# A spectral filter's channel mixing moved from the whole matrix array to 64x64 tiles of it

## The reference

```
h = layer_norm(x, n1_g, n1_b)
xf = rfft2(h, axes=(1, 2), norm='ortho')          # 128 x 65 frequencies, 128 channels
xf = xf.reshape(B, H, W//2+1, 8, 16)              # 8 blocks of 16 channels
o1r = relu(xr @ w1[0] - xi @ w1[1] + b1[0])       # each block with its own 16x16 weights
o1i = relu(xi @ w1[0] + xr @ w1[1] + b1[1])
o2r = softshrink(o1r @ w2[0] - o1i @ w2[1] + b2[0])
o2i = softshrink(o1i @ w2[0] + o1r @ w2[1] + b2[1])
h = irfft2(o2r + 1j * o2i) + h + x
out = gelu(layer_norm(h, n2_g, n2_b) @ mw1 + mb1) @ mw2 + mb2 + h
```

## Time and profile before

| What | Value |
|---|---|
| Time, median of 3 runs | 1652.82 us (1651.64 to 1653.29) |
| Time of the profiled execution | 1653.2 us |
| Its span, first to last instruction | 1651.4 us |
| Mean granted TensorE clock | 1.000 |
| First filter, start of `dft_h` to start of `idft_h` | 77.67 to 170.36 us |
| Last filter | 1273.5 to 1366.3 us |

### The profile page before, as it was taken

One profiled execution on the slowest core, in us unless ns is written; L12 is line 12 of the kernel. 1 busy time (PEld: TensorE's weight loads), 2 busy tenths in 40 slices (PEclk: granted clock), 3 DMA queues, 4 the chain that ended last, 5 costly groups with the idle time before them and its releaser, 6 DMA issues.

```text
span 1651.4 us, 34968 instructions
## 1 busy us (share of the span) xinstructions
PE 1598.6 (97%) x11278; PEld 1445.4 (88%) x11278; DVE 1076.1 (65%) x2697; ACT 938.4 (57%) x1782; POOL 619.8 (38%) x774
## 2 busy tenths in 40 slices
PE   0999999999999999999999999999999999999999
PEld 0999988888999988888899998888889998888888
DVE  7889566556559856655656966665664995555453
ACT  5655276666535546666644545666663553666665
POOL 4800046766800016676660002677673000211111
PEclk9999999999999999999999999999999999999999
DMA  7500713333300062333320042333331006011111
GB/s 222 197 15 1 238 45 108 95 102 121 97 14 1 8 236 83 108 95 102 122 78 1 1 166 94 101 108 101 102 110 46 1 1 204 27 32 38 32 39 45
DMA packets 167249, 137.67 MB, mean 83 GB/s; under 512 B 9459, under 2 KB 131189, under 8 KB 167157
## 3 DMA queue, kind: packets, MB, share of 16 engines
q1 hardware_dynamic: 166354, 136.23, 26.1%
q10 hardware_dynamic: 802, 0.21, 0.1%
HBM read 69.29 MB, written 67.11 MB: 83 GB/s over the span
## 4 chain that ended last, share of the span: by engine, by line
PE 79%; DVE 14%; issue 4%; ACT 1%; SPq 1%; DVEq 1%; DMA 1%; POOL 0%; ACTq 0%
PE ps L756 27%; PE ps L558 7%; PE ps L722 7%; PE ps L724 7%; PE ps L683 7%; PE ps L723 7%; DVE vsb L1105 4%; PE ps L716 3%; PE ps L702 3%; PE ps L708 3%; DVE csb L1107 3%; DVE usb L1095 3%; DVE usb L1096 2%; PE ps L568 2%; PE ps L612 2%
## 5 line engine op out<-in xcount | busy, mean ns | idle before, releaser
L756 PEld LDWEIGHTS ps<-mw,gel 128*128 128x128 f32 x4000 | 520.6, 191 | 42.3
L756 PE MATMUL ps<-mw,gel 128*128 128x128 f32 x4000 | 523.7, 274 | 0.0
L875 ACT ACTIVATE gel<-ps,mb1f 128x512 f32<-128x512 f32 x500 | 343.7, 687 | 250.5 <-PE ps L724 219.7
L1460 POOL TENSOR_TENSOR arena<-arena,mb2rep 128x512 f32<-128x512 f32 x125 | 160.1, 1281 | 654.6 <-ACT hn L861 654.6
L722 PE MATMUL ps<-hth,mw1h 128*128 128x512 f32 x512 | 260.3, 508 | 2.9 <-DVE htl L1206 1.5
L1449 POOL TENSOR_SCALAR arena<-xnext,rstd,shift 128x128 f32<-128x128 f32 x360 | 159.3, 462 | 207.6 <-DVE shift L1344 207.6
L861 ACT ACTIVATE hn<-arena,shift,rstd 128x128 f32 (+1 forms) x512 | 221.7, 483 | 16.7 <-DVE shift L1344 16.7
L1189 DVE TENSOR_TENSOR arena<-ps,arena 128x512 f32 (+1 forms) x60 | 41.5, 691 | 252.4 <-PE ps L708 233.8
L724 PE MATMUL ps<-hth,mw1l 128*128 128x512 f32 x512 | 202.1, 395 | 0.0
L723 PE MATMUL ps<-htl,mw1h 128*128 128x512 f32 x512 | 200.8, 392 | 0.0
L846 ACT ACTIVATE osb<-usb,vectors 128x512 f32<-128x512 f32 (+1 forms) x136 | 95.6, 703 | 158.3 <-DVE usb L1096 158.3
(11 more groups left out here) (118 smaller groups left out, 2397.9 us busy)
## 6 DMA issues: line engine op xcount, KB each, us to landing
arena<-aside SPq DMA_DIRECT2D x128, 256.0 KB, 5.0
aside<-gz SPq DMA_DIRECT2D x96, 256.0 KB, 3.0
between<-xout SPq DMA_DIRECT2D x62, 256.0 KB, 2.3
out_dram<-xout SPq DMA_DIRECT2D x62, 256.0 KB, 2.3
xnext<-between SPq DMA_DIRECT2D x60, 256.0 KB, 3.1
aside<-first SPq DMA_DIRECT2D x32, 256.0 KB, 2.3
xnext<-in_x_dram SPq DMA_DIRECT2D x30, 256.0 KB, 3.1
first<-in_x_dram SPq DMA_DIRECT2D x1, 960.0 KB, 7.2
```

What stands on the lines that cost most here:

```text
L756: mm = pe.matmul(ps[:, r % 2, P * i:P * i + P], gel[:, r % 2, m, P * i:P * i + P], mw2[:, s // IMAGES, m, :], start=(m == 0 and i == 0), s ...
L875: act.activation(gel[:, r % 2, m, :], ps[:, 2 + m % 2], ACT.Gelu, bias=mb1f[:, s // IMAGES, m:m + 1]).then_inc(gelu_out, 1)
L1460: pool.tensor_tensor(t, t, b, ALU.add).then_inc(mb2_done, 1)
```

## The change

`mix1` and `mix2` take two units (both halves of the channels) at once, and each matmul uses a part of the array.

The channels are laid out anew: a half of 64 channels is split in two quarters `g` of 32, so that partitions 0 to 63 hold real and imaginary part of one quarter, and 64 to 127 those of the other. In `mix1` each of the four combinations of `q` and `g` has a stationary operand of 64x64 on a tile of the array of its own: rows `g`, columns `g ^ q`. The even and odd parts are no longer combined by VectorE. Four groups of such matmuls write the sums directly into PSUM: even to the first 65 columns, even again to the other 63, odd added to the columns 1 to 63, and odd with the other sign added to the last 63. `w1s` has four kinds of weights instead of two, for the signs.

`e_copy`, `combine`, `usb` and `nyq` go. `o_relu` reads PSUM. `mix1` of a pair waits for both relus of the pair before. In `mix2` the stationary operand is the upper or lower 64 rows of `osb` (64x128), with 64 moving columns, into banks 4 + 2 (p % 2) + `g`; the banks alternate by pair. `filter_` issues for each pair: `mix1` of the next, `mix2` of this one, two `dft_h`. Other parts: the small loads of the weights are 13 (`load_weights`) and 5 (`load_vectors`) transfers instead of 6, GpSimd builds two more kinds of weights, `scale_spectral` scales four kinds, and the evictions of `dft_w` write to the new layout.

The diff, cut to its core:

```
...
+PAIRED = UNITS // 2
+EDGE_PAIR = 4
...
-        w1s = sb("w1s", [P, 2, 2, 2, HALF])
-        w2s = sb("w2s", [P, 2, 2, HALF])
+        w1s = sb("w1s", [P, 4, 2, 2, QUART])
+        w2s = sb("w2s", [P, 2, 2, QUART])
...
-            dst = spec_of(s)[:, :, q, :, bass.ds(GROUP * cg, GROUP)]
+            dst = spec_of(s)[:, :, q, g ^ q, :, bass.ds(GROUP * cg, GROUP)]
...
+            def mix1(s, p):
+
+                alone = p == 1
                 if not alone:
+                    pe.wait_ge(g_out, 2 * BATCHES * s + spectrum_of(2 * p + 1) + 1)
+                if p:
+                    pe.wait_ge(o_out, UNITS * s + 2 * p)
+
+                def quarters(j0, j1, depth, src, dst, kind, start=False):
+
+                    for q in range(2):
+                        for g in range(2):
+                            own_rows = slice(HALF * g + depth[0], HALF * g + depth[1])
+                            cols = slice(HALF * (g ^ q), HALF * (g ^ q) + HALF)
+                            to = ps[cols, 2 + q].rearrange("p (j k) -> p j k", j=GROUP)[:, j0:j1]
+                            mm = pe.matmul(to[:, :, dst[0]:dst[1]], w1s[own_rows, kind, q].rearrange("p r c -> p (r c)"),
+                                           gsb[own_rows, q, j0:j1, src[0]:src[1]], start=start, stop=True,
                                                skip_group_check=True)
+                    return mm
+
+                def sums(j0, j1, depth, even, plus, minus, start=False):
+
+                    quarters(j0, j1, depth, (0, EVEN), (0, EVEN), even, start)
+                    quarters(j0, j1, depth, (1, KWS), (EVEN, P), even)
+                    quarters(j0, j1, depth, (EVEN, P), (1, KWS), plus)
+                    return quarters(j0, j1, depth, (EVEN, P), (EVEN, P), minus)
+
                 if alone:
+                    mm = sums(0, 1, (QUART, HALF), 1, 3, 0, True)
+                elif p:
+                    mm = sums(0, GROUP, (0, HALF), 0, 1, 2, True)
+                else:
+                    sums(1, GROUP, (0, HALF), 0, 1, 2, True)
+                    sums(0, 1, (0, QUART), 0, 1, 2)
...
+            def mix2(s, p):
+                kws = 1 if p == 1 else GROUP
...
+                if p >= 2:
+                    pe.wait_ge(v_out, UNITS * s + 2 * p - 2)
+                for q in range(2):
+                    pe.wait_ge(o_out, UNITS * s + 2 * p + q + 1)
+                    for i in range(kws):
+                        for g in range(2):
+                            own_rows = slice(HALF * g, HALF * (g + 1))
+                            at_ = 2 * HALF * 2 * q + HALF * i
+                            mm = pe.matmul(ps[:, 4 + 2 * (p % 2) + g, at_:at_ + HALF], osb[own_rows, q, i, :],
+                                           w2s[own_rows, q].rearrange("p r c -> p (r c)"), start=True, stop=True)
+                mm.then_inc(m2_mm, 2)
...
+                for p in range(PAIRED):
+                    if p + 1 < PAIRED:
+                        mix1(s, p + 1)
...
+                    mix2(s, p)
+                    if p == EDGE_PAIR:
                         edges(s)
+                    if p + 3 < PAIRED:
+                        for q in range(2):
+                            dft_h(s, 2 * p + 6 + q)
...
-            def e_copy(s, n, q, kws=GROUP):
...
-                act.activation(dst, src, ACT.Relu, bias=b1v[:, q:q + 1]).then_inc(o_out, 1)
+                act.activation(dst, ps[:, 2 + q, 0:P * kws], ACT.Relu, bias=b1v[:, q:q + 1]).then_inc(o_out, 1)
...
                 def batch(b, last=False):
                     n = 2 * b + 2
...
                     if not last:
+                        for q in range(2):
+                            g_copy(s, n + 2 + q, q)
+                    for q in range(2):
+                        o_relu(s, n + q, q)
...
-                    for kind in range(2):
+                    for kind in range(4):
...
-            def combine(s, n, q, kws=GROUP):
...
```

More of the change, by code:

```diff
@@ L527, in dc_bias @@
                 for q in range(2):
-                    mm = pe.matmul(ps[:, 7, q:q + 1], w1s[0:HALF, 0, q].rearrange("p r c -> p (r c)"),
-                                   beta64[0:HALF, q:q + 1], start=(q == 0), stop=True, skip_group_check=True)
-                mm.then_inc(dc_mm, 1)
+                    if q:
+                        pe.wait_ge(dc_mm, 2 * n + 1)
+                    for g in range(2):
+                        rows_, cols = slice(HALF * g, HALF * g + QUART), slice(HALF * (g ^ q), HALF * (g ^ q) + HALF)
+                        mm = pe.matmul(ps[cols, 7, q:q + 1], w1s[rows_, 0, q].rearrange("p r c -> p (r c)"),
+                                       beta64[q][rows_], start=(q == 0), stop=True, skip_group_check=True)
+                    mm.then_inc(dc_mm, 1)
             def evicted(s, cg):
@@ L576, in mix1 @@
                 if not alone:
[L577 to L586, removed]
@@ L602, in mix1 @@
                         mm = pe.matmul(ps[:, 2 + q, 0:1], IDENT, dcbias[:, q:q + 1], start=False, stop=True,
                                        skip_group_check=True)
[L604 to L614, removed]
+                mm.then_inc(m1_mm, 2)
@@ L625, in filter_ @@
                 mix1(s, 0)
[L626 to L640, removed]
-                        edges(s)
+                for q in range(2):
+                    dft_h(s, 4 + q)
+                for p in range(PAIRED):
+                    if p + 1 < PAIRED:
+                        mix1(s, p + 1)
+                    if p == EDGE_PAIR + 1:
+                        pe.wait_ge(y_done, (UNITS + 1) * s + 2 * EDGE_PAIR + 2)
+                    mix2(s, p)
+                    if p == EDGE_PAIR:
+                        edges(s)
+                    if p + 3 < PAIRED:
+                        for q in range(2):
+                            dft_h(s, 2 * p + 6 + q)
+                if s:
+                    fc1_held(s, 0)
+                    fc1_held(s, 1)
+                else:
+                    pe.wait_ge(v_out, UNITS * s + UNITS - 2)
+                    keep_warm(8, 6)
             def edges(s):
                 pe.wait_ge(t_edge, s + 1)
+                pe.wait_ge(v_out, UNITS * s + 2 * EDGE_PAIR)
                 for i, m in enumerate((REVERSE, IDENT)):
@@ L907, in _ @@
                 for q in range(2):
-                    with act.Fori(0, CGROUPS // 8) as j:
-                        for r in ((0, 2) if s else range(4)):
-                            a_out(s, q, j, r)
+                    for g in range(2):
+                        with act.Fori(0, CGROUPS // 16) as j:
+                            for r in ((0, 2) if s else range(4)):
+                                a_out(s, q, g, j, r)
                 if s:
@@ L1249, in _, with batch @@
                     for q in range(2):
[L1250 to L1252 removed]
+                        for g in range(2):
+                            with dve.Fori(0, CGROUPS // 16) as j:
+                                for r in (1, 3):
+                                    a_out(s, q, g, j, r)
                         if q == 0 and s % IMAGES == 0:
                             scale_spectral(s // IMAGES)
[L1255 to L1263 removed]
+                for q in range(2):
+                    shrink(s, q, 0, q, 0)
+                for q in range(2):
+                    shrink(s, 2 + q, BATCHES, q, 1, kws=1)
                 edges(s)
[L1266 removed]
+                def batch(b, odd):
                     for q in range(2):
[L1268 to L1278 removed]
+                        shrink(s, 2 * b + 2 + q, b, q, odd)
+                        if isinstance(b, int) and b + 1 == EDGE_PAIR and q == 0:
+                            edges_out(s)
+                for b in range(1, EDGE_PAIR):
+                    batch(b, (b + 1) % 2)
+                with dve.Fori(EDGE_PAIR // 2, BATCHES // 2 - 1) as i:
+                    own.enter(i, 4, EDGE_PAIR // 2)
+                    for h in range(2):
+                        batch(2 * i + h, 1 - h)
+                own.leave(BATCHES // 2 - 1)
+                batch(BATCHES - 2, 1)
+                batch(BATCHES - 1, 0)
                 dve.wait_ge(y_done, (UNITS + 1) * (s + 1))
```

174 lines of the change are left out of this document (66 added, 108 removed).

## The result

The changed kernel takes 1697.24 us (median of 4 runs, 1695.81 to 1698.33) against 1653.05 us for the kernel before (median of 4 runs), a ratio of 1.0268 with a 95% interval of 1.025 to 1.0286. It is slower by 44 us, not by the 134 us forecast. The direction was right and the range, 300 us wide, held the time, but the forecast of the size was wrong by a factor of three.

What follows compares the result with a forecast made beforehand. TensorE and VectorE tie at 2.65 us a repeat. A pair goes from 5.30 to 1.78 + 3.40 + 1.78 + 0.36 = 7.32 us, +129 over 64 pairs; 1653.2 + 129 + 4 + 1 = 1787 us, range 1615 to 1915.

Steps and rivals of the forecast that it cites:

- the term of mix1: mix1 of each pair: tiles run two at a time, never four, so 3.40 us a pair.
- rival (b): mix1: four tiles at once, 1.70 us, mix2 at 1.78; pair 5.62 us, +20 us, 1679 us; chance 0.12.
- the likeliest case alone: Whole kernel: forecast of 7.3 us a pair, 1755 to 1820 us by changes of shape and head; chance 0.36.
- Rival (a): mix2: its 32 weight loads run one after another, 3.55 us; pair 9.09 us, +243 us, 1901 us; chance 0.22.
- Changes of shape: TensorE between dft_h, mix1 and mix2: three changes a pair at 0.12 us each, 0.36 us a pair.
- the ring: mix1 waits for both relus of the pair before, behind gsb copies: 6.0 us a pair, below TensorE's 7.32.
- I had +1: Head of each filter: extra small matmuls less shorter waits, -3 to +5 us, taken as +1 a filter.

Runs made afterwards that it cites:

- The first experiment: Changed kernel with mix1's 16 matmuls of a pair reordered, all four of one tile before those of the next: 1875.0 us.
- the third experiment: Changed kernel with mix1 of the full pairs in eight 128x128 matmuls on the whole array, output not the reference's: 1789.04 us.
- the sixth experiment: Changed kernel with mix2 on four 64x64 tiles, each 64x128 operand of osb cut in two: 1629.36 us, ratio 0.9859.
- The second: Changed kernel with mix2's loop over the row half g outside the one over the four columns: 1742.32 us.
- the fourth run: Changed kernel with both mix1 and mix2 of the full pairs on the whole array, output not the reference's: 1764.03 us.
- The fillers: Changed kernel with matmuls on unused data in the gaps at each filter's end: 1690.27 us, ratio 1.023.
- seventh: Changed kernel with mix2 on four 64x64 tiles and matmuls on unused data at the filter's end: 1632.54 us, ratio 0.9877.
- eighth: Changed kernel with only mix2 of the full pairs on the whole array, mix1 on its tiles, output not the reference's: 1682.02 us, ratio 1.0175.

## Why the prediction was wrong in its size

**The step that failed** is the term of mix1: "the second starts only when the first is through ... two at a time, never four", 3.40 us. Measured 1.87 us, of which 0.17 is the change of shape: four at a time. The first half of that step is right: the second instruction of a matmul does wait for the first. The second half is wrong: while it waits, it doesn't hold up the matmuls behind it. The first instructions of four matmuls start together (the view of L611 above), though the fourth of them is the seventh instruction in the order of the program. The first experiment shows that holding up begins later: by the rule that is drawn from it, at a second waiting matmul of one tile. The changed kernel's order never has that. The starts in the earlier trace rows could not tell, for there all matmuls go to the same cells. The step is worth 64 x (3.40 - 1.70) = 109 us of the forecast's 134, and rival (b), which had it right, stood at 0.12 with 1679 us. The direction is not owed to the failed step, for (b) is slower than before as well. (By its own terms the likeliest case alone begins at 1748 us, not 1755: 0.36 x 64 = 23 and 4 x 4 = 16 below 1787. Nothing hangs on it.)

**Four at once, and in which order.** What the Trainium skill's page TensorEngine Tiling (Array Packing), "Theoretical Speedup", gives, up to 2x for each of two small dimensions, so four tiles at once, was right here: 1.87 us with the change of shape, where one tile at a time would be 6.80. (The whole array takes 3.53 us in the third experiment because each of its matmuls there does the work of two tiles.) The Trainium skill's page TensorE: Matmul & The Clock Gate, "The mechanism", says that matmuls start and end in the order of the program. The starts measured here are not so, and the measurement decides: in the changed kernel the first instructions of four float32 matmuls start before any second one, and in the first experiment the second tile's first matmul starts at 117.1 us, when the first tile's fourth, which stands ahead of it, still waits. That a waiting instruction blocks the queue was my addition.

**mix2** was 1.93 us, 1.78 plus the change of shape, as taken: loads two at a time at 0.111. That loads bound it is shown by the sixth experiment: each tile still has 16 instructions of 64 moving columns, only the columns of a load are halved, and mix2 takes 1.04 us. The second shows that loads run in pairs all the way only if the row halves alternate. Rival (a), serial loads, falls.

**Changes of shape** cost more than the 0.12 us taken from the earlier trace rows: dft_h, mix1 and mix2 each last 0.20, 0.17 and 0.15 us longer than their work, 0.52 a pair, and the fourth run, without changes, shows the bare 1.79 us. The term was 0.36; the difference is 10 us in all, and with the 7 us of the filters' ends (below) it is what rival (b)'s 1679 us lack. 0.52 is also just about what the pair got longer (0.49): apart from the changes of shape, TensorE's work in a pair did not become more.

**VectorE and ScalarE** behaved as said: shrink 3.8 us a pair, the relu from PSUM 685 ns against the 687 taken, no wait for the ring in the steady part, and TensorE waiting for the relu only at the filter's end.

**What the forecast did not have** is the end of the filter. Without dft_h too little covers the relus there, TensorE stands for 1.46 and 0.94 us (the timeline of the last filter of the kernel after, idle time and releaser in brackets), and the granted clock falls to 0.50 at the ends of all four filters.

```profile
1399.00 1.94 PE L611 MATMUL ps<-gsb,w1s 64*64 64x260 f32 x32 [1.46 <-ACT osb L877]
...
1403.81 2.55 PE L648 MATMUL ps<-w2s,osb 64*128 64x64 f32 x32 [0.94 <-ACT osb L877]
```

The fillers give back 7 us of the 44. With them the filter is 101.8 us: 92.8, plus 16 x 0.49 = 7.8, plus 1.2, which is the head and the rest of the tail; I had +1. The account over the program: 31 us in the full pairs, 7 that the fillers give back by the clock, some 5 in heads and tails (4 x 1.2), together 43 of 44.

**What stays open.** The gaps alone don't make the clock fall. The sixth kernel has the same gaps at the filter's end (1.57 and 0.95 us), and its clock doesn't fall there; nor does that of the fourth (1.45 and 0.93 us). In the runs with mix2 on half arrays and no fillers (the changed kernel and the first three experiments) it fell near the ends of the filters, all but the first filter of the third; in those without such a mix2 (the fourth, sixth, seventh and eighth) it did not. A short fall some 33 us after the end of the first filter is another matter: the first, third, sixth, seventh and eighth experiment have it. Which property of that mix2 matters was not tried, and neither was what separates the two rules for the queue.

## What to carry to other kernels

Before packing small matmuls into tiles, add up how long one tile works and how many loads of weights each row half needs, and let neighbours in the program go to different tiles. Keep successive blocks in the same shape: three changes in a pair of 5.8 us are all that made TensorE's pair longer here. Giving mix2 mix1's 64x64 shape turned +44 us into -23, by 0.89 us a pair in mix2, whose loads have half the columns, and 0.11 us in mix1, for a change of shape less. And where two engines are full at once, relief of one is worth nothing until the other gets shorter as well.

## What the runs showed of the hardware

Four 64x64 tiles in float32 give full value: the 32 instructions of a pair, of 252 or 260 columns each, take 1.70 us plus the change of shape, no longer than one tile needs for its eight. A change of the array's shape costs about 0.17 us on average (0.52 us for three in a pair, 0.35 for two). Weight loads of 64 rows go side by side with those of the other 64 rows: 32 loads of 128 columns in 1.78 us, against 3.55 at 0.111 us each. 64x64 loads on all four tiles do too: 64 loads and 64 matmul instructions were issued in 1.04 us. The order counts: four matmuls of one tile before those of the next made mix1 4.61 us instead of 1.87. That a tile takes one waiting matmul and a second one holds up all tiles is drawn from these starts, not shown against the other rule.
